# A quantised pair of layers rewritten, a product given to GpSimd, one step of a pass turned later, and a loop written out

## The reference, cut to what matters

```python
x = x + L0_attn(layernorm(x))      # 16 heads of 64; its output is itself normalised with ln_gamma, ln_beta
x = x + L0_xattn(layernorm(x), ctx)   # 64 rows of context, weights rounded
x = x + L0_ffn(layernorm(x))       # grouped: each sequence has its own W1 (1024x256) and W2 (256x1024), no nonlinearity
x = x + L1_attn(layernorm(x))      # 8 experts, top 2 of 8, ternary weights
x = x + L1_xattn(layernorm(x), ctx, mask)
x = x + L1_ffn(layernorm(x))       # the quantised pair

def _L0_attn_ref(...):             # its end
    y = o @ w_proj + b_proj + x
    y = (y - mean) * rsqrt(var + EPS) * ln_gamma + ln_beta

def quant_act_uint8(x):            # the quantised pair; round() to whole steps
    s = max(max(x), EPS) / 255     # one step for the whole tensor
    return clip(round(x / s), 0, 255) * s, s
def quant_weight_int8_perchannel(w):
    s = max(max(abs(w), axis=1), EPS) / 127
    return clip(round(w / s), -128, 127) * s, s
def quant_linear(x, w, b):
    xq, s_in = quant_act_uint8(x); wq, s_w = quant_weight_int8_perchannel(w)
    return xq @ wq.T + round(b / (s_in * s_w)) * (s_in * s_w)
h = relu(quant_linear(x, w1, b1))  # 1024 hidden columns
return quant_linear(h, w2, b2)
```

## Time and profile before

| | |
|---|---|
| median of 3 runs | 2395.47 us (2390.36 to 2404.99) |
| the profiled execution's own time | 2393.87 us |
| its span in the trace | 2392.2 us |
| PE, busy share of the span | 71% |
| VectorE | 67% |
| ScalarE | 57% |
| GpSimd | 34% |
| granted PE clock, mean | 0.855 of full speed |

### The profile page before, as it was taken

One profiled execution on the slowest core, in us unless ns is written; L12 is line 12 of the kernel. 1 busy time (PEld: TensorE's weight loads), 2 busy tenths in 40 slices (PEclk: granted clock), 3 DMA queues, 4 the chain that ended last, 5 costly groups with the idle time before them and its releaser, 6 DMA issues. The chain is left out here.

```text
span 2392.2 us, 43530 instructions
## 1 busy us (share of the span) xinstructions
PE 1696.3 (71%) x13405; PEld 1078.5 (45%) x13405; DVE 1606.5 (67%) x3129; ACT 1374.0 (57%) x2171; POOL 817.9 (34%) x751
## 2 busy tenths in 40 slices
PE   4889898989899898985899802223454677774855
PEld 1455555555555555553677601211222355553323
DVE  6867777787878778775233386735773767675774
ACT  3788888888878798881454412433553323333543
POOL 0434545454445454451000050570001444451042
PEclk9999999999999999996798955556666888987778
DMA  6222222222222222222122111422112111111002
GB/s 179 61 50 61 60 53 63 61 50 63 61 50 63 57 60 56 61 48 96 36 71 72 36 75 53 151 78 88 53 35 71 38 33 23 30 26 47 0 1 71
DMA packets 173941, 139.90 MB, mean 58 GB/s; under 512 B 83808, under 2 KB 155539, under 8 KB 173506
## 3 DMA queue, kind: packets, MB, share of 16 engines
q1 hardware_dynamic: 166850, 122.91, 19.8%
q0 software_dynamic: 6912, 14.71, 2.8%
HBM read 62.05 MB, written 20.97 MB: 35 GB/s over the span
## 5 line engine op out<-in xcount | busy, mean ns | idle before, releaser
L588 ACT ACTIVATE a_p_hi<-ps,a_probs_up,a_s_scale 128x512 f16<-128x512 f32 x512 | 397.9, 777 | 79.8 <-ACTq L586 79.2
L589 ACT ACTIVATE a_probs<-ps,a_probs_up,a_s_scale 128x512 f32<-128x512 f32 x512 | 398.4, 778 | 0.0
L690 DVE TENSOR_REDUCE a_top<-ps 128x2 f32<-128x1024 f32 x256 | 312.7, 1221 | 121.5 <-DVEq L689 121.5
L914 POOL TENSOR_TENSOR a_p_lo<-a_probs,a_p_hi 128x1024 f16<-128x1024 f32 x128 | 284.8, 2225 | 179.3 <-POOLq L913 163.9
L902 POOL TENSOR_TENSOR a_ops<-a_ident_down,a_top 64x256 f16<-64x256 f32 x256 | 158.8, 620 | 395.9 <-POOLq L897 387.4
L699 DVE TENSOR_TENSOR a_p_lo<-a_probs,a_p_hi 128x1024 f16<-128x1024 f32 x128 | 184.6, 1443 | 37.2 <-DVEq L698 37.2
L452 PE MATMUL ps<-a_ops 128*128 128x512 f16 x512 | 196.3, 383 | 13.5 <-PEq L450 13.5
L471 PE MATMUL ps<-a_v_hi,a_p_hi 128*128 128x65 f16 x2048 | 203.2, 196 | 2.2 <-PEq L466 2.2
L438 PE MATMUL ps<-a_qk,a_qd 128*128 128x512 f16 x512 | 153.4, 381 | 72.2 <-PEq L436 72.2
L474 PE MATMUL ps<-a_v_lo,a_p_hi 128*128 128x64 f16 x2048 | 203.2, 194 | 0.0
L475 PE MATMUL ps<-a_v_hi,a_p_lo 128*128 128x65 f16 x2048 | 203.0, 195 | 0.0
(11 more groups left out here) (482 smaller groups left out, 3782.2 us busy)
## 6 DMA issues: line engine op xcount, KB each, us to landing
a_ops<-a_qk SPq DMA_DIRECT2D x384, 128.0 KB, 2.4
f_w<-in_L_ffn_W_dram SPq DMA_DIRECT2D x16, 1024.0 KB, 7.4
a_qd<-a_qk SPq DMA_DIRECT2D x128, 64.0 KB, 2.3
g_a<-in_L_attn_gp_w_dram SPq DMA_DIRECT2D x8, 1024.0 KB
X<-in_x_dram SPq DMA_DIRECT2D x8, 512.0 KB, 9.9
expert_in<-g_w SPq DMA_DIRECT2D x8, 512.0 KB
g_a<-in_L_attn_dp_w_dram SPq DMA_DIRECT2D x8, 512.0 KB
e_x_in<-expert_in SPq DMA_DIRECT2D x8, 512.0 KB, 4.3
```

Of the source, the lines that this page charges most:

```text
L588: nc.scalar.activation(p_hi[:, h % 2, k, :], scores, ACT.Exp, bias=probs_up[:], scale=s_scale[:])
L589: nc.scalar.activation(probs[:, h % 2, k, :], scores, ACT.Exp, bias=probs_up[:], scale=s_scale[:]).then_inc(st_taken, 1)
L690: nc.vector.tensor_reduce(top[:, c % 2, 2 * pair:2 * pair + 2], ps[:, ROW:ROW + 2, :], AX.X, ALU.max).then_inc(row_taken, 1)
L914: nc.gpsimd.tensor_tensor(p_lo[:, h % 2, 2:KT, :], probs[:, h % 2, 2:KT, :], p_hi[:, h % 2, 2:KT, :], ALU.subtract).then_inc(p_made_pool, 1)
```

## The change

Four parts; one of them is a whole stage.

1. **Self-attention.** In batches 1 to 7, VectorE no longer makes `z` in one instruction (28 times). It writes minus the mean of the tile (`less_mean`, 128x1), and ScalarE makes `y - mean` one head later, at heads 4, 6, 8 and 10, behind that head's exponentials and ahead of the next batch's `normalise`. GpSimd multiplies by gamma, two tiles at once, at heads 8 and 12. VectorE waits for that at head 13. The last batch's end keeps `centre` on VectorE.

2. **Middle.** `f_rows` of batch b-1 stands behind `scores(b + 1)` and `w2`'s last two turns, not ahead of them; on ScalarE `f_rows_out` stands behind `w2_out(b, 2)` and `w2_out(b, 3)`; `in_order` is altered to match.

3. **Masked attention.** The four `Fori` loops become Python loops, so that the 7 turns are written out. SyncE's list gets the loads of the pair's weights (`next_weights.load`, 2 MB in two transfers, and two small ones) behind its own.

4. **The pair.** The weights are there at its start. VectorE takes the weights' peaks first, then the row moments; of each batch's 4 normalised tiles it makes 3 and ScalarE 1; the weights' rounding and turning stand between the turning of rows; `b2` and `unit2` are kept as columns, one number for each partition, so the row forms, `ones`, `unit2_diag` and GpSimd's two jobs are gone. In the second pass PE makes the hidden tile (b, c) and then two products of `outputs(b - 1, c)`, now turned round: `w2T` is the stationary side and 512 rows of `h8` stream. The output comes out transposed; ScalarE writes one half of `outT` with scale and bias (at c = 4), VectorE the other (at c = 0 of the next batch), PE turns it back (`turn_back`, 8 transposes, at c = 2), and VectorE adds it to `X` from PSUM (`add_x`, at c = 3). SyncE stores each batch when it is done; `store_block` is gone. All loops are written out.

```diff
 # self_attention, ScalarE
+                def centre(t):
+                    act.wait_ge(y_means, 1)
+                    act.sem_inc(y_means, -1)
+                    nc.scalar.activation(z[:, t, :], y[:, t, :], ACT.Identity, bias=less_mean[:, t:t + 1])
+                    if t % 2:
+                        act.drain().then_inc(y_centred, 1)
...
                         for k in range(2, KT):
                             powers(h, k)
+                        if finish and h - 2 in PROJ_B:
+                            centre(PROJ_B[h - 2])
 # self_attention, VectorE
-                            centre(t)
+                            nc.vector.tensor_scalar(less_mean[:, t:t + 1], ln_y.mean_var[:, t, 0:1], -1.0, None, ALU.mult)
+                            dve.drain().then_inc(y_means, 1)
+                        if finish and h == 13:
+                            dve.wait_ge(z_made, 2)
+                            dve.sem_inc(z_made, -2)
 # self_attention, GpSimd
+                def times_gamma(half):
+                    pool.wait_ge(y_centred, 1)
+                    pool.sem_inc(y_centred, -1)
+                    nc.gpsimd.tensor_tensor(z[:, halves[half], :], z[:, halves[half], :], each(gam), ALU.mult)
+                    pool.drain().then_inc(z_made, 1)
...
+                        if finish and h in (8, 12):
+                            times_gamma((h - 8) // 4)
 # middle, TensorE
-                    if b:
-                        for c in range(DC):
-                            f_rows(b - 1, c)
                     if b + 1 < B:
                         scores(b + 1, bank_of["scores", b + 1])
                     if b < B:
                         turn_w2(b, 2)
                         turn_w2(b, 3)
+                    if b:
+                        for c in range(DC):
+                            f_rows(b - 1, c)
 # middle, ScalarE
+                    if b < B:
+                        w2_out(b, 2)
+                        w2_out(b, 3)
                     if b:
                         for c in range(DC):
                             f_rows_out(b - 1, c)
-                    if b < B:
-                        w2_out(b, 2)
-                        w2_out(b, 3)
 # masked_attention, SyncE and the loops of the four engines
+                next_weights.load(sp)
-                with pe.Fori(0, B - 1) as b:
+                for b in range(B - 1):
 # quantised_pair, SyncE
+                for b in range(B):
+                    sp.wait_ge(rows_done, 1)
+                    sp.sem_inc(rows_done, -1)
+                    sp.dma_start(rows[:, b * TT:(b + 1) * TT, :], X[:, b * TT:(b + 1) * TT, :]).then_inc(stored, 16)
 # quantised_pair, TensorE, second pass
-                hidden_again(0)
-                with pe.Fori(0, B // 2 - 1) as pair:
-                    for j in range(2):
-                        hidden_again(pair * 2 + j + 1)
-                        outputs(j)
-                hidden_again(B - 1)
-                outputs(0)
-                outputs(1)
+                def outputs(b, n):
+                    m = n // 4
...
+                    for c in (2 * (n % 4), 2 * (n % 4) + 1):
+                        last = nc.tensor.matmul(ps[:, OUT + m, :], w2T[:, c, m * P:(m + 1) * P], h8[:, b % 2, c, :],
+                                                start=(c == 0), stop=(c == FC - 1))
...
+                for b in range(B + 1):
+                    for c in range(FC):
+                        if b < B:
+                            hidden_again(b, c)
+                        if b >= 2 and c == BACK_AT:
+                            turn_back(b - 2)
+                        if b:
+                            outputs(b - 1, c)
+                turn_back(B - 1)
 # quantised_pair, ScalarE, second pass
+                def outputs_out():
+                    act.wait_ge(out_full, 1)
+                    act.sem_inc(out_full, -1)
+                    nc.scalar.activation(outT[:, 0, :], ps[:, OUT, :], ACT.Identity, scale=unit2[:, 0:1], bias=b2_col[:, 0:1]).then_inc(out_taken, 1)
+                    act.drain().then_inc(outT_act, 1)
 # quantised_pair, VectorE, second pass
-                nc.vector.tensor_scalar(unit2_row[:], unit2_row[:], h_unit[:], None, ALU.mult)
+                nc.vector.tensor_scalar(unit2[:], unit2[:], h_unit[:], None, ALU.mult)
...
+                for b in range(B + 1):
+                    for c in range(FC):
+                        if b < B:
+                            round_hidden(b, c)
+                        if b >= 2 and c == 0:
+                            outputs_out()
+                        if b >= 2 and c == BACK_AT + 1:
+                            add_x(b - 2)
+                outputs_out()
+                add_x(B - 1)
```

More of the change, by code:

```diff
@@ L2702, in _ @@
                 power(0)
-                with act.Fori(0, B - 1) as b:
+                for b in range(B - 1):
                     sequence(more=True)
@@ L2792, in _ @@
                 maximum(0, 1)
-                with dve.Fori(0, B - 1) as b:
+                for b in range(B - 1):
                     sequence(b, more=True)
@@ L2910, in _ @@
[L2910 to L2921 removed]
+                pe.wait_ge(w_out, 2)
@@ L2922, in _ @@
+                pe.sem_inc(w_out, -2)
+                for b in range(B):
                     pe.wait_ge(x8_made, 1)
@@ L3066, in _ @@
                 dve.sem_inc(a_taken, FC)
-                with dve.Fori(0, B) as b:
+                for b in range(B):
                     for c in range(FC):
@@ L3124, in _ @@
[L3124 to L3133 removed]
+                nc.vector.tensor_tensor(b2_col[:], b2_col[:], unit2[:], ALU.mult)
+                dve.drain().then_inc(out_scales_made, 1)
```

443 lines of the change are left out of this document (246 added, 197 removed).

## The result

The changed kernel takes 2374.2 us (median of 14 runs, 2365.05 to 2378.05) where the one before takes 2395.94 beside it (14 runs): a ratio of 0.9905, 95% interval 0.9888 to 0.9921. It is about 1% faster. The prediction had 2338, and a range of 2314 to 2366 that doesn't hold it. Of a forecast gain of 57 us, 22 came.

The account below looks back on a forecast made before the run. No engine bounds the whole; PE is dense in self-attention, the pair is mostly chains of waits. Terms -10.5 - 15.9 - 9.3 - 10.0 - 2 - 5 - 5 = -57.7 gave span 2334.5, time 2338 us, range 2314 to 2366.

Parts of the forecast that it names:

- The clock in masked attention: Masked attention: writing out the loops saves the jumps in seven turns, -5 us, bounds -10 and 0.
- The middle: Middle stage: PE's idle moves ahead of the outputs, +4.6, and some low clock comes back; -2 us, bounds -10 and +6.
- I count half of 14.8 back and 0.8 lost: Middle stage: of 14.8 us lost to low clock in two steps, 7.4 returns; a new idle costs 0.8.
- if a step of the middle stage loses its clock where none did before: Middle stage: a sign, named beforehand, that the forecast is wrong.
- Self-attention: Moving z off VectorE gains -5 us, bounds -12 and +8; ScalarE adds 0.2 at heads 4 and 5, 0.45 at 6 and 7.
- that rival: Self-attention: GpSimd's 14 products by gamma each stop VectorE and PE waits, +17 us, 2355; chance 0.06.
- The rival of ScalarE as the bound: Self-attention: each of 28 new ScalarE instructions puts 0.7 on the path, +20 us instead of -5, 2363; chance 0.17.
- The pair: Pair and stores: -45.7 us in all; start -10.5, second pass's first batch -15.9, its rest -9.3, stores -10.0; first pass unchanged.
- the rest of the second pass: Pair, after the first batch: period falls from about 9.9 to 8.5 us; -9.3, bounds -13 and +1.
- The rival of the falling clock in this pass: Pair's second pass: PE waits for ScalarE's buffers, the clock falls, periods stay 9.9; +10 us, 2348; chance 0.13.
- The loads: Masked attention's start: 2 MB of new loads priced at 0, bound +3; as rival, colliding with gathers, +5, 2343, chance 0.05.
- The rival of the other sign: Self-attention: ScalarE's centre waits for VectorE's mean, 2.1 us at each of 28, +59, 2397 and over; chance 0.03.

Follow-up runs that it names:

- only_masked_written_out: The kernel before with only masked attention's four loops written out, without the loads of the pair's weights: 2413.7 us, ratio 1.0064.
- masked_loop_back: The changed kernel with masked attention's four hardware loops put back, all else kept: 2353.0 us, ratio 0.9831 to the kernel before.
- pair_outputs_later: The changed kernel with the outputs of a batch in the pair's second pass issued one hidden tile later: 2373.2 us, ratio 0.9901 to the kernel before.
- only_pair: The kernel before with the new pair alone, its loads in masked attention's first part: 2354.6 us, ratio 0.9833.
- middle_back: The changed kernel with the middle stage's old order put back: 2364.6 us, ratio 0.9873 to the kernel before.
- gamma_back: The changed kernel with self-attention as before, VectorE making z in one instruction: 2381.0 us, ratio 0.9942 to the kernel before.
- masked_filled: The changed kernel, masked attention written out, with transposes of the identity that compute nothing where PE idles: 2335.6 us, ratio 0.9746 to the kernel before.

## Why the prediction was wrong

**The clock in masked attention** is the step that failed. The prediction priced the written-out loops at "Seven turns of 0.55 and 0.2 for the other engines' jumps", so at -5 with bounds of -10 and 0, and left the granted clock out of this stage's sum, though it had weighed it in the middle and in the pair. The term itself was right: with the clock held the turn is 0.5 shorter (35.5 and 35.0), and at 0.91 it is 37.0 and 37.5. But in most turns the low clock went from 6.8 to 17 us, and a written-out turn takes 40.9 instead of 37.0: 3.9 lost, 3.4 of it net of the jump. No bound of this term lay above zero. The 24.6 us in the traces, 18 to 21 in the medians (only_masked_written_out, masked_loop_back), are what put the time outside the range: without them it is 2353 to 2356. That the rest would lie inside is in part luck: self-attention's gain came out 10 us larger than forecast, and covers the 6.3 and 5.6 that the middle and the pair fell short. Why the clock falls a second time in the written-out turn isn't shown.

**The middle** was weighed rightly in its parts and wrongly in its sum. The 0.85 us by which ScalarE delays the outputs is 1.0 a step at the full clock (25.06 for 24.06), the idle moved as told and is 3.05, where 2.5 was said. "I count half of 14.8 back and 0.8 lost" failed: both long steps went, but the clock now falls in every step of the trace, which costs 1.8 to 2.5 each (26.9 and 27.6 for 25.06). +4.3 in the traces against -2. Over all traces without filler in that stage, the seven with the new order have 272.5 to 275.7, and of the five with the old one four have 268.2 to 268.8 and one 278.6; by the medians it costs 5 to 10. The prediction had named this sign itself, "if a step of the middle stage loses its clock where none did before", and gave it 0.8 us.

**Self-attention** was a gain of 12 to 15, not 5. The direction and the mechanism held: PE's waits for VectorE ahead of `rows` are 26 us less. What was mis-sized is ScalarE's part: "+0.2 at heads 4 and 5, +0.45 at 6 and 7". By the starts of a head's first key tile (line 452, now 441), in the fourth batch, heads 4 and 5 together moved by -0.8, 6 and 7 by +0.3 (-0.7 and +0.9), 8 and 9 by -0.6, and 10 by -0.8: -2.0 where the prediction had -0.7 (the seven batches have -0.8 to -3.4, with a mean of -2.0). Head 4 gains what VectorE gives back, and ScalarE's instruction of 0.51 costs nothing there; only head 7 is longer, behind that instruction and the two of `normalise`. GpSimd's product took 1.27, and VectorE was not held up by it to a degree that the stage shows; that rival had no run of its own. The rival of ScalarE as the bound, 0.17 of the chance, is refuted.

**The pair** came within its bounds: -40.1 for -45.7. Start -11.9 for -10.5; first batch -16.2 for -15.9; stores -9.5 for -10.0; the first pass -0.7. The term that was off is the rest of the second pass, -1.7 for -9.3. I took 8.5 for the period and it is 9.30; "PE is the densest at 7.9", and what stands on top is 1.36 of waiting for VectorE's last rounding, where 0.6 was put; pair_outputs_later shows that this wait isn't the only thing that holds the period. Six periods (five of 9.30 and one of 8.6) are 4 over the 51 of the prediction. The other 3 us are at the ends: 10.5 to the first turning back and 7.0 from the seventh of eight to the last addition, 17.5 where 14.0 was put. A slip in that term: with a period of 9.9 the sum comes to -0.9, not to the +1 of its bound, and the rival to +8.4 and not +10. The rival of the falling clock in this pass didn't come: the clock is at 1.00 from 2286 to 2360, up to the last turning back.

**The loads** beside the gathers cost little: the stage has 352.0 in only_pair, 349.5 before, and the term had 0 to 3.

**The rival of the other sign** named a wait and not the clock. What could end slower stood in the windows of masked attention, which the prediction didn't read: a mean clock of 0.91, that is a low stretch in each turn, whose length an edit of the turn's idles can change.

## What to carry to other kernels

Where a stage repeats one turn and its mean clock lies between the two levels, the turn's length is a function of how much low clock it has, and an edit that moves or removes a half microsecond of idle can move that either way. Price such an edit at both: here 34.5 and 40.9 for the same turn. Then take the choice away: fill PE's longest idles with products that nothing reads. It cost 36 transposes a turn and gave back 39 us, more than any of the four edits in this change but one. Read the trace after it: in the middle stage, with its new order, 24 transposes a step left one or two steps of 30.9 in two of three traces.

Look at each part alone before calling a change good: two of four parts here cost time, and the best one alone (2354.6) did as well as all without the worst (2353.0).

## What the runs showed of the hardware

A turn can lock into one pattern of the clock and keep it: the changed kernel's last five turns have 40.9 to 41.0 us at 0.79, those of masked_loop_back 37.5 to 37.6 at 0.91. The six traces with the turns written out and no filler in them all end in turns of 40.9 to 41.0, the four with all loops in turns of 37.5 to 37.6. But the path there differs: middle_back has a turn of 36.9 first, and gamma_back goes through 34.5, 37.0 and 40.9 with the same instructions. The changed kernel's 14 runs lie within 13 us, so repeated runs agree and don't warn of it.

Idle alone didn't tell which pattern it would be. The longest wait in a turn was 3.96 us before and 3.30 in the changed kernel, and the one at the turn's border 1.42 and 0.87; the kernel with the longer ones had the higher clock:

```profile
2067.49 0.66 PE L2562 MATMUL ps<-ident,x_o 128*128 128x128 f32 x2 [3.96 <-PEq L2560]
```

and, changed:

```profile
2030.75 0.66 PE L2578 MATMUL ps<-ident,x_o 128*128 128x128 f32 x2 [3.30 <-PEq L2576]
2044.49 1.94 PE L2562 MATMUL ps<-ident,x_s 128*128 128x128 f32 x8 [0.87 <-PEq L2560]
```

The last row is the border: the same 8 products took 1.07 before and take 1.94, since they now lie in the second low stretch.

With both filled, the clock was 1.00 through whole turns (window of masked_filled above). The Trainium skill (TensorE: Matmul & The Clock Gate, "HAM oscillation — how this bites in real kernels") tells of a kernel whose clock falls anew in every tile of its loop because PE waits there; that waits are behind the low stretches here agrees, since products that nothing reads, put into the waits, took the low stretches out of five turns in a row.
